# Fused two-layer conditional block on Trainium2: moving the raw score pairs from a batch's first half-steps to its later ones

## The chip, the cores and the metric

One Trainium2 chip, one of its cores. The metric is device time in microseconds (us) of one execution. TensorE is called PE, VectorE DVE, ScalarE ACT, GpSimd POOL, and SyncE (which issues most DMAs) SP.

## What is computed

The input is x (8 batches, 512 tokens, width 256) and a condition vector per batch. Two layers follow each other:

```
layer 0:  h = x * (scale(cond) * rsqrt(mean(x*x)+eps)); u = h @ up_w.T; val, gate = split(u)
          y = act_quant(val * gelu(gate)) @ weight_quant(down_w).T + x
layer 1:  x = y + a_alpha * attention(gamma * rmsnorm(y) + beta)          # 16 heads of 16
          out = x + f_alpha * (silu(n @ gate_w.T) * (n @ hidden_w.T) @ out_w.T + out_b),
                n = gamma' * rmsnorm(x) + beta'
```

Attention is softmax(q k^T / 4) v over all 512 keys.

## The kernel before

**Phase 1** is layer 0, tile by tile (32 tiles of 128 tokens). It ends near 262 us and the change does not touch it.

**Phase 2** is layer 1, one batch after the other. A batch is a table of 32 half-steps, h = 0 to 31 (HALVES). The heads are worked in four groups g of four heads; eight half-steps make a group, and two half-steps a tile of 128 keys. In every half-step PE does an *excursion* (excursion_pe, L1218): two score matmuls (score_pe, L923; keys by queries, 512 columns) for the softmax of the current batch, and the two halves of one *raw pair* (raw_pe, L882). A raw pair is the product of q and k for 128 queries of two heads without any shift, into the one two-bank PSUM tensor raw_pair. DVE reduces it to row maxima (maximum_dve, L890), and eight raw pairs (RAWS) complete a group: shift_dve (L896 to L902) turns the maxima into rows, and SP writes them with eight small DMAs into two rows of q_stack (shift_sp, L912), so that the score matmul subtracts the maximum itself. There is only one raw_pair tensor: raw_pe of pair n waits until DVE has read pair n-1 (raw_read). A score matmul uses 50 rows of the array in one half of it, and the raw half beside it 48 rows of the other half; the code alternates halves (1 - x).

Raw pairs run ahead of the scores: half-step h works on pair h + AHEAD, and AHEAD is 11; pair 32 is pair 0 of the next batch. Pair 16 is the first of the second pair of groups: it needs all twelve stacking DMAs of the batch (semaphore stacked[1]; eight issued by SP, four by ACT in h = 2 and 3, stack_act).

In the even half-steps PE also does values_pe (L942, probabilities times values of the previous key tile). Behind the excursion stands the half-step's entry in the table (plan, L1162): h 0 q and k projection of the second stack (qk_pe, L808); h 1 and h 4 the two halves of the value product (v_pe, L858, V_AT); h 2 and 3 the output projection of the batch before (wo_pe, L1003); h 7 the transposes of its normalised rows (xf_pe, L1059); h 8 and 9 q and k of the first stack of the next batch; h 10 to 25 alternately gate and hidden product of its feed-forward part (hidden_pe, L1091); h 26 to 31 its out product (out_pe, L1135, six entries of 12 or 24 matmuls). Every entry uses one of the two banks ab, whose release (pair_free) by DVE it waits for.

The other engines follow the same table one half-step later, each in its own fixed order. Around the change:

- DVE h 5: mean_dve (L1034), then the maximum, then normed_dve (L1044, four tensor_scalar of 128x256 that write the normalised rows for the transposes of h 7; semaphore xn3_done). v_dve (L865) copies a value half out of its bank first thing in the half-step after the product; xf_dve (L1068) follows the transposes in h 8 and waits for q_in_low, the split of the next batch's input, since both use x_in.
- ACT h 5: split_xa_act (L531) after the exps (exp_act, L931); POOL h 5: rstd_pool (L1038), split_xa_pool (L545). The place is SPLIT_XA_AT = V_AT[1] + 1. xf_act and xf_pool (L1081) and bias_pool (L1051) come at h 8.
- DVE h 8n: sums_dve (L955), h 8n+1: divide_dve (L961, L964); gate_dve (L1103) and product_dve (L1110) finish each gate and hidden product, and product_dve of a half-step stands before its maximum.

Batch 0 has no feed-forward part before it; its odd half-steps without an entry hold three filler matmuls (fill_pe, L1208). Batches 1 to 5 are a loop, 6 and 7 are written out; batch 7 has no following batch, so its raw pairs end with h 20. After it comes a tail for its own feed-forward part. Batches 1 to 6 are called the loop batches here.

Of the kernel before, what the change touches and what calls it, by code (L numbers as in the profile page):

```python
# [5 lines left out]
def cond_seq_kernel(nc, x_tok, xT, condT, vec_wT, up_wT, down_wT, wqT, wkT, wvT, woT, gate_wT, hidden_wT,  # L6
# [25 lines left out]
    G = 4  # L32
# [14 lines left out]
    with ctx:  # L47
# [161 lines left out]
        xn3_done = sem("xn3_done")  # L209
# [660 lines left out]
        def raw_at(b, n):  # L870

            return b + n // (RAWS * G), n % (RAWS * G) // RAWS, n % RAWS

        def raw_pe(pe, b, g, e, half):

            slot, qt = 2 * g + e // T, e % T
            if half == 1:
                if e == 0 and g % 2 == 0:
                    pe.wait_ge(stacked[g // 2], (b + 1) * STACK)
                pe.wait_ge(raw_read, credited(raw_read, b * (RAWS * G) + (RAWS * g + e)))  # L880
            rows = slice(64 * half, 64 * half + ROWS)
            mm = nc.tensor.matmul(raw_pair[:, half, :], q_stack[rows, slot, qt * P:(qt + 1) * P],  # L882
                                  k_stack[rows, slot, :], start=True, stop=True)
            if half == 0:
                mm.then_inc(raw_full, 1)
# [266 lines left out]

        V_AT, WO_AT, XF_AT, FFN_AT, OUT_AT = (1, 4), 2, 7, 10, 26
        Q_AT, K_AT, TO_STACK = 8, 9, 16
        SPLIT_XA_AT = V_AT[1] + 1
        OUT_PIECES = ([(0, 0)], [(2, 0)], [(0, 1)], [(1, 0), (1, 1)], [(2, 1)], [(3, 0), (3, 1)])
# [3 lines left out]
        def plan(ffn, following):  # L1162

            table = [[] for _ in range(HALVES)]
            table[0] = [("qk", 1, 0), ("qk", 1, 1)]
            for m in range(2):
                table[V_AT[m]] = [("v", m)]
            if following:
                table[Q_AT] = [("qk", 0, 0)]
                table[K_AT] = [("qk", 0, 1)]  # L1170
            if ffn:
                table[WO_AT] = [("wo", 0), ("wo", 1)]
                table[WO_AT + 1] = [("wo", 2), ("wo", 3)]
                table[XF_AT] = [("xf",)]
                for f in range(NH):
                    table[FFN_AT + 2 * f] = [("gate", f)]
                    table[FFN_AT + 2 * f + 1] = [("hidden", f)]
                for n, pieces in enumerate(OUT_PIECES):
                    table[OUT_AT + n] = [("out", t, half) for t, half in pieces]
            return table  # L1180
# [12 lines left out]
        def both(u, stage):  # L1193

            return tuple(u + n for n in stage)
# [15 lines left out]
        BEFORE = 1  # L1211
        USES_FIRST, USES_LOOP = uses(False, 2)[1], uses(True, 2)[1]

        def last_of(b, g):

            return (b, g - 1) if g > 0 else (b - 1, G - 1)

        def excursion_pe(pe, b, h, following):  # L1218

            g, kt = h // 2 // T, h // 2 % T  # L1220
            rb, rg, e = raw_at(b, h + AHEAD)
            raws = following or h + AHEAD < RAWS * G
            for x in range(2):
                score_pe(pe, b, g, kt, 2 * (h % 2) + x)
                if raws:
                    raw_pe(pe, rb, rg, e, 1 - x)

        def pe_batch(pe, b, u, ffn, following):
            table, at = plan(ffn, following), uses(ffn, following)[0]
            for h in range(HALVES):  # L1230
                excursion_pe(pe, b, h, following)
                n = h // 2
                if h % 2 == 0 and (n > 0 or ffn):
                    pb, pg = last_of(b, n // T) if n % T == 0 else (b, n // T)
                    values_pe(pe, pb, pg, (n - 1) % T, both(u, at["v"]) if n in (1, 1 + HALF) else None)
                if not ffn and not table[h] and h % 2 == 1:
                    fill_pe(pe, h, u, at)
                for p in table[h]:
                    if p[0] == "qk":
                        qk_pe(pe, b if p[1] == 1 else b + 1, p[1], p[2], u + at[f"qk{p[1]}"][p[2]])  # L1240
                    elif p[0] == "v":
                        v_pe(pe, b, p[1], u + at["v"][p[1]])
                    elif p[0] == "wo":
                        wo_pe(pe, b - 1, p[1], u + at["wo"][p[1] // HALF])
                    elif p[0] == "xf":
                        xf_pe(pe, b - 1, both(u, at["xf"]))
                    elif p[0] == "out":
                        out_pe(pe, b - 1, p[1], p[2], u + at["out"])
                    else:
                        hidden_pe(pe, b - 1, 0 if p[0] == "gate" else 1, p[1], u + at["hidden"])  # L1250
# [33 lines left out]

        def dve_batch(dve, b, u, ffn, following):
            table, at = plan(ffn, following), uses(ffn, following)[0]
            for h in range(HALVES + 1):
                g = h // 2 // T
                done = table[h - 1] if h > 0 else []
                for p in done:  # L1290
                    if p[0] == "v":
                        v_dve(dve, b, p[1], u + at["v"][p[1]])
                    elif p == ("qk", 1, 1):
                        qk_dve(dve, 1, 1, 4 * b + 2)
                    elif p[0] == "wo" and p[1] % HALF == HALF - 1:
                        wo_dve(dve, b - 1, p[1] // HALF, u + at["wo"][p[1] // HALF])
                        if p[1] == T - 1:
                            x2_dve(dve, b - 1, 1, u + at["wo"][1])
                    elif p[0] == "xf":
                        xf_dve(dve, b - 1, both(u, at["xf"]), b + 2 if following else b + 1)  # L1300
                    elif p[0] == "hidden":
                        product_dve(dve, b - 1, p[1], u + at["hidden"])
                    elif p[0] == "out" and p[1] % HALF == HALF - 1 and p[2] == 1:
                        out_dve(dve, b - 1, p[1] // HALF, u + at["out"])
                if ffn and h == WO_AT + 3:
                    mean_dve(dve, b - 1)
                if h < HALVES and (following or h + AHEAD < RAWS * G):
                    rb, rg, e = raw_at(b, h + AHEAD)
                    maximum_dve(dve, rb, rg, e)
                    if e == RAWS - 1:  # L1310
                        shift_dve(dve, rb, rg)
                if ffn and h == WO_AT + 1:
                    x2_dve(dve, b - 1, 0, u + at["wo"][0])
                if ffn and h == WO_AT + 3:
                    normed_dve(dve, b - 1)
                for p in done:
                    if p[0] == "gate":
                        gate_dve(dve, b - 1, p[1])
                    elif p[0] == "qk" and p[1] == 0:
                        qk_dve(dve, 0, p[2], 4 * b + 4)  # L1320
                if h < HALVES and h % 8 == 0 and (g > 0 or ffn):
                    sums_dve(dve, *last_of(b, g))
                if h == 0 and ffn:
                    divide_dve(dve, *last_of(b, g))
                if h == 0:
                    qk_dve(dve, 1, 0, 4 * b + 2)
                if h == 0 and ffn:
                    turn_dve(dve, b - 1, GP - 1)
                if h % 8 == 1 and g > 0:
                    divide_dve(dve, b, g - 1)  # L1330
                if h % 8 == 2 and g == 2:
                    turn_dve(dve, b, 0)

        def pool_batch(pool, b, u, ffn, following):
            table, at = plan(ffn, following), uses(ffn, following)[0]
            for h in range(HALVES + 1):
                g = h // 2 // T
                done = table[h - 1] if h > 0 else []
                if ffn and h == 1:
                    normalise_pool(pool, b - 1, GP - 1)  # L1340
                if g == 2 and h % 8 == 2:
                    normalise_pool(pool, b, 0)
                if ffn and h == WO_AT + 3:
                    rstd_pool(pool, b - 1)
                if following and h == SPLIT_XA_AT:
                    split_xa_pool(pool, b + 1)
                if ffn and h == XF_AT + 1:
                    xf_pool(pool, b - 1)
                    bias_pool(pool, b - 1)
                for p in done:  # L1350
                    if p[0] == "hidden":
                        product_pool(pool, b - 1, p[1])
                    elif p[0] == "out" and p[1] % HALF == HALF - 1 and p[2] == 1:
                        out_pool(pool, b - 1, p[1] // HALF, u + at["out"])
# [201 lines left out]
```

## Time and profile before

| | us |
|---|---|
| median of 3 runs | 1066.9 (1066.33 to 1073.98) |
| the profiled execution | 1072.98 |
| its span, first to last instruction | 1071.2 |
| mean granted clock of TensorE in it | 0.952 |
| PE busy / DVE busy / ACT busy / POOL busy | 1004.5 / 759.0 / 537.0 / 271.8 |

Busy shares are means over stages with different limits. The granted clock is a share of 2.4 GHz and has two levels here, 1.0 and 0.5. All start times below are us from the first instruction. Records of one engine overlap by about 0.1 us, so the step from one start to the next is the better price.

### The profile page before, as it was taken

What the parts mean: (1) busy time and instruction counts of PE and PEld (TensorE: products, weight loads), DVE (VectorE), ACT (ScalarE), POOL (GpSimd) and SP (SyncE); (2) the same over time, 40 slices, a digit from 0 to 9 for tenths busy, and PEclk for the clock granted to TensorE, in tenths of its full rate; (3) what the DMA queues carried; (4) which work ended last, traced back from release to release, by engine and by line L of the source; (5) the groups of instructions that cost most, each with busy time, mean ns of one, the idle gap of its engine ahead of it and who ended that gap; (6) DMA issues with size and microseconds to landing.
All of it is one profiled execution on the core that took longest, in us unless ns stands there. A gap on an engine that the chain in (4) does not pass through costs nothing.

```text
span 1071.2 us, 17062 instructions
## 1 busy us (share of the span) xinstructions
PE 1004.5 (94%) x5380; PEld 619.5 (58%) x5380; DVE 759.0 (71%) x1208; ACT 537.0 (50%) x1119; POOL 271.8 (25%) x260
## 2 busy tenths in 40 slices
PE   5999999996999899999989999998999899999868
PEld 4777777774434455545645564565556456645656
DVE  5888788995667786777577767867776776785232
ACT  4466455443555555446355535644564564456221
POOL 1265422220000321222122213212221321122133
PEclk9999999996999899979989998999999899999879
DMA  9545574442321220313024031302221230310000
GB/s 285 136 103 131 139 163 113 109 104 60 109 61 42 69 66 2 79 50 64 13 67 106 8 78 51 65 11 69 71 43 45 66 65 3 80 36 1 25 0 21
DMA packets 93685, 75.11 MB, mean 70 GB/s; under 512 B 44848, under 2 KB 79736, under 8 KB 93632
## 3 DMA queue, kind: packets, MB, share of 16 engines
q1 hardware_dynamic: 79040, 57.20, 20.4%
q10 hardware_dynamic: 14592, 17.25, 6.9%
q8 instruction: 27, 0.44, 0.2%
q14 instruction: 26, 0.21, 0.1%
HBM read 27.73 MB, written 12.61 MB: 38 GB/s over the span
## 4 chain that ended last, share of the span: by engine, by line
PE 81%; DVE 10%; issue 4%; DMA 2%; SPq 1%; ACT 1%; POOL 0%; DVEq 0%; POOLq 0%; ACTq 0%
PE bank L1091 19%; PE bank L358 13%; PE bank L923 11%; PE bank L942 10%; PE bank L1135 9%; PE raw_pair L882 5%; PE bank L808 5%; DVE rowmax L890 3%; PE bank L1003 3%; PE bank L381 2%; DVE amax L440 1%; PE bank L858 1%; PE bank L1059 1%; DVE x_in L1044 1%; SPq L912 1%
## 5 line engine op out<-in xcount | busy, mean ns | idle before, releaser
L890 DVE TENSOR_REDUCE rowmax<-raw_pair 128x2 f32<-128x1024 f32 x256 | 312.9, 1222 | 132.3 <-PE raw_pair L882 132.3
L931 ACT ACTIVATE probs<-bank 128x512 f32<-128x512 f32 x512 | 281.7, 596 | 231.3 <-PE bank L923 229.4
L923 PE MATMUL bank<-q_stack,k_stack 50*128 50x512 f32 x512 | 198.2, 458 | 2.4 <-DMA q_stack<-shift_rows 1.3
L358 PE MATMUL bank<-up_w,xs_part 128*128 128x512 f32 x768 | 193.8, 405 | 6.7 <-issue 5.3
L882 PE MATMUL raw_pair<-k_stack,q_stack 48*128 48x512 f32 x512 | 178.1, 472 | 21.9 <-DVE rowmax L890 21.3
L358 PEld LDWEIGHTS bank<-up_w,xs_part 128*128 128x128 f32 x768 | 143.7, 192 | 41.9 <-issue 8.5
L942 PE MATMUL bank<-probs,v_ext 128*17 128x512 f32 x1024 | 141.9, 627 | 0.3
L1121 POOL TENSOR_TENSOR hid<-scratch,hid 128x512 fp32r<-128x512 f32 x64 | 82.5, 1288 | 225.9 <-ACT hid L1117 225.9
L923 PEld LDWEIGHTS bank<-q_stack,k_stack 50*128 50x128 f32 x512 | 82.0, 191 | 88.1 <-issue 52.5
L1091 PE MATMUL bank<-xf_part,gate_w 128*128 128x512 f32 x384 | 108.0, 417 | 4.9 <-POOL xf_part L1081 4.2
L1091 PEld LDWEIGHTS bank<-xf_part,gate_w 128*128 128x128 f32 x384 | 68.8, 192 | 68.2 <-issue 51.5
L1135 PEld LDWEIGHTS bank<-out_w,hid 128*128 128x128 f32 x768 | 91.9, 188 | 25.6 <-issue 25.0
L1091 PE MATMUL bank<-xf_part,hidden_w 128*128 128x512 f32 x384 | 106.7, 413 | 0.0
L1135 PE MATMUL bank<-out_w,hid 128*128 128x256 f32 x768 | 100.6, 285 | 0.0
L882 PEld LDWEIGHTS raw_pair<-k_stack,q_stack 48*128 48x128 f32 x512 | 71.7, 191 | 41.1 <-DVE rowmax L890 36.3
L1091 PEld LDWEIGHTS bank<-xf_part,hidden_w 128*128 128x128 f32 x384 | 68.6, 190 | 33.0 <-issue 20.4
L288 ACT ACTIVATE gelu<-bank,rstd 128x512 f32<-128x512 f32 x64 | 44.0, 688 | 58.7 <-PE bank L358 58.7
L1099 ACT ACTIVATE scratch<-bank 128x512 f32<-128x512 f32 x64 | 38.2, 597 | 67.9 <-PE bank L1091 67.9
L410 DVE SCALAR_TENSOR_TENSOR h<-bank,rstd,gelu 128x512 f32<-128x512 f32 x64 | 47.7, 746 | 23.0 <-PE bank L358 23.0
L336 POOL TENSOR_TENSOR xs_part<-xs,xs_part 128x256 fp32r<-128x256 f32 x32 | 23.6, 739 | 147.1 <-DVE ms L403 126.7
L1103 DVE SCALAR_TENSOR_TENSOR scratch<-scratch,bank 128x512 f32<-128x512 f32 x64 | 43.4, 679 | 21.3 <-ACT scratch L1099 21.3
L982 POOL TENSOR_TENSOR split<-o_sb,split 128x512 fp32r<-128x512 f32 x16 | 20.5, 1282 | 130.5 <-ACT split L978 130.5
(121 smaller groups left out, 1108.6 us busy)
## 6 DMA issues: line engine op xcount, KB each, us to landing
q_stack<-split SPq DMA_DIRECT2D x48, 128.0 KB, 2.9
q_stack<-hid SPq DMA_DIRECT2D x48, 128.0 KB, 2.9
xk<-xT SPq DMA_DIRECT2D x32, 128.0 KB, 2.9
xt<-x_tok SPq DMA_DIRECT2D x32, 128.0 KB, 2.7
x_spill<-x1t ACTq DMA_DIRECT2D x32, 128.0 KB, 2.5
xa_spill<-xa ACTq DMA_DIRECT2D x32, 128.0 KB, 2.3
x_in<-xa_spill SPq DMA_DIRECT2D x8, 512.0 KB, 4.9
k_stack<-split ACTq DMA_DIRECT2D x32, 128.0 KB, 4.8
```

The source lines that it names most:

```text
L288: nc.scalar.activation(gelu[:, j, :], gate_bank[j][:], ACT.Gelu, scale=rstd[:, m % 2:m % 2 + 1]) \
L358: last = nc.tensor.matmul(bank[j][:], xs_part[a][:, m % 2, k, :], up_w[w][:, k, col + j * W:col + (j + 1) * W], start=(i == 0), stop=(i == ...
L410: nc.vector.scalar_tensor_tensor(h[:, j * W:(j + 1) * W], val_bank[j][:], rstd[:, m % 2:m % 2 + 1], gelu[:, j, :], ALU.mult, ALU.mult) \
L808: last = nc.tensor.matmul(bank[:], weight[wp][:, k, m * P:(m + 1) * P], xa_part[a][:, k, :], start=(i == 0), stop=(i == 5))
L882: mm = nc.tensor.matmul(raw_pair[:, half, :], q_stack[rows, slot, qt * P:(qt + 1) * P], k_stack[rows, slot, :], start=True, stop=True)
L890: nc.vector.reduce_max(rowmax[:, e:e + RAWS + 1:RAWS], raw_pair[:], AX.X).then_inc(raw_read, 1)
L923: nc.tensor.matmul(score_bank[c % 3][:], k_stack[rows, slot, kt * P:(kt + 1) * P], q_stack[rows, slot, :], start=True, stop=True).then_inc ...
L931: nc.scalar.activation(probs[:, (kt % 2) * J + j, :], score_bank[c % 3][:], ACT.Exp).then_inc(exp_done, 1)
L942: last = nc.tensor.matmul(o_bank[32 * j:32 * j + HD + 1, :], v_ext[:, kt, J * g + j, :], probs[:, (kt % 2) * J + j, :], start=(kt == 0), s ...
L1091: last = nc.tensor.matmul(ab[n][:], weight[wp][:, k, f * P:(f + 1) * P], xf_part[a][:, k, :], start=(i == 0), stop=(i == 5))
L1121: nc.gpsimd.tensor_tensor(hid[1][:, f, :], scratch[1][:], hid[0][:, f, :].bitcast(f32), ALU.subtract) \
L1135: last = nc.tensor.matmul(ab[m][:, (t % HALF) * D:(t % HALF + 1) * D], hid[a][:, f, t * P:(t + 1) * P], out_w[wp][:, f, :], start=(i == 0) ...
```

## The change

Three edits.

1. Raw pairs get a table of their own. None in h 0 to 4 and in h 6; two in h 12 and in h 22, 24, 26, 28 and 30; one in all others. Since each batch now starts with pair 16, a batch hands the next one 16 finished pairs rather than 11. In batch 0 the half-steps 0 to 4 keep theirs (the table starts at 11), so it does 37 raw pairs; batch 7 does 16. The first pair of a half-step stays inside the excursion; the second comes after values_pe, both halves one behind the other, ahead of the table's entry.
2. The second value product moves from h 4 to h 5, and with it v_dve to h 6 and the input split (ACT and POOL) from h 5 to h 6.
3. normed_dve moves from h 5 to h 6, and POOL's split waits for it.

```
-        V_AT, WO_AT, XF_AT, FFN_AT, OUT_AT = (1, 4), 2, 7, 10, 26
+        V_AT, WO_AT, XF_AT, FFN_AT, OUT_AT = (1, 5), 2, 7, 10, 26
+        RAW_PAIRS = [0] * 5 + [1, 0] + [1] * 5 + [2] + [1] * 8 + [1, 2] * 5 + [1]
+        def raw_table(first, following):
+            pairs = [1] * (2 * RAWS - AHEAD) + RAW_PAIRS[2 * RAWS - AHEAD:] if first else RAW_PAIRS
+            start = AHEAD if first else 2 * RAWS
+            table = [list(range(start + sum(pairs[:h]), start + sum(pairs[:h + 1]))) for h in range(HALVES)]
+            return [[n for n in numbers if following or n < RAWS * G] for numbers in table]
...
-        def excursion_pe(pe, b, h, following):
+        def excursion_pe(pe, b, h, raws):
             g, kt = h // 2 // T, h // 2 % T
-            rb, rg, e = raw_at(b, h + AHEAD)
-            raws = following or h + AHEAD < RAWS * G
             for x in range(2):
                 score_pe(pe, b, g, kt, 2 * (h % 2) + x)
-                if raws:
-                    raw_pe(pe, rb, rg, e, 1 - x)
+                for n in raws[:1]:
+                    raw_pe(pe, *raw_at(b, n), 1 - x)
...
                     values_pe(pe, pb, pg, (n - 1) % T, both(u, at["v"]) if n in (1, 1 + HALF) else None)
+                for n in raws[h][1:]:
+                    for half in (1, 0):
+                        raw_pe(pe, *raw_at(b, n), half)
...
-                if h < HALVES and (following or h + AHEAD < RAWS * G):
-                    rb, rg, e = raw_at(b, h + AHEAD)
+                for n in raws[h] if h < HALVES else []:
+                    rb, rg, e = raw_at(b, n)
                     maximum_dve(dve, rb, rg, e)
...
-                if ffn and h == WO_AT + 3:
+                if ffn and h == WO_AT + 4:
                     normed_dve(dve, b - 1)
...
                 if following and h == SPLIT_XA_AT:
+                    if ffn:
+                        pool.wait_ge(xn3_done, b)
                     split_xa_pool(pool, b + 1)
```

## Rows read from the trace of the kernel before

**Rows 1.** The page: busy time, and the group of the exps.

```profile
PE 1004.5 (94%) x5380; PEld 619.5 (58%) x5380; DVE 759.0 (71%) x1208; ACT 537.0 (50%) x1119; POOL 271.8 (25%) x260
...
L931 ACT ACTIVATE probs<-bank 128x512 f32<-128x512 f32 x512 | 281.7, 596 | 231.3 <-PE bank L923 229.4
```

**Rows 2.** Windows, first and last of six loop batches: length, busy per engine, granted clock, DMA share, GB/s.

```profile
338.79:435.80 97.01, 93.47 (x532) 53.59 (x528) 70.54 (x94) 50.01 (x97) 23.02 (x17) 0.95 0.21 52
...
822.68:918.28 95.60, 92.12 (x533) 52.79 (x529) 70.64 (x94) 49.74 (x98) 23.68 (x18) 0.96 0.20 50
```

**Rows 3.** Windows inside one loop batch (h 0 at 532.00, gate product at 567.00).

```profile
548.16:556.00 7.84, 4.55 (x21) 1.70 (x21) 6.48 (x10) 3.71 (x6) 3.46 (x2) 0.75 0.01 2
556.00:567.00 11.00, 11.00 (x50) 5.54 (x49) 7.64 (x10) 5.83 (x11) 4.88 (x3) 0.71 0.20 58
567.00:628.84 61.84, 61.84 (x362) 36.14 (x358) 43.16 (x56) 31.80 (x60) 12.83 (x10) 1.00 0.18 44
```

**Rows 4.** Timeline, same batch, h 4 to 8: start, length, instruction, idle before it.

```profile
546.54 1.69 PE L858 MATMUL bank<-wv,xa_part 128*128 128x256 f32 x12
...
548.16 0.73 PE L882 MATMUL raw_pair<-k_stack,q_stack 48*128 48x512 f32 x2
...
548.55 0.66 DVE L865 TENSOR_SCALAR v_ext<-bank 128x512 f32<-128x512 f32 x1
...
549.67 1.06 ACT L531 ACTIVATE xa_part<-x_in 128x1024 fp32r<-128x1024 f32 x1
550.42 3.24 DVE L1044 TENSOR_SCALAR x_in<-x,rstd 128x256 f32<-128x256 f32 x4
...
550.48 0.59 PE L882 MATMUL raw_pair<-k_stack,q_stack 48*128 48x512 f32 x2 [1.34 <-DVE rowmax L890]
...
550.81 2.44 POOL L545 TENSOR_TENSOR xa_part<-x_in,xa_part 128x1024 fp32r<-128x1024 f32 x1 [0.42 <-ACT xa_part L531]
...
554.85 0.88 PE L882 MATMUL raw_pair<-k_stack,q_stack 48*128 48x512 f32 x2 [1.95 <-DVE rowmax L890]
...
558.32 1.53 DVE L1068 TENSOR_SCALAR x_in<-bank,par 128x512 f32<-128x512 f32 x2 [0.95 <-PE bank L1059]
```

**Rows 5.** Timeline of batch 7: no input split; no raw pairs after h 20.

```profile
934.75 1.14 DVE L1044 TENSOR_SCALAR x_in<-x,rstd 128x256 f32<-128x256 f32 x4
...
943.96 2.28 DVE L964 TENSOR_TENSOR o_pair<-o_tok,inv_sum 128x256 f32<-128x256 f32 x1
...
976.17 0.49 PE L923 MATMUL bank<-q_stack,k_stack 50*128 50x512 f32 x2
976.59 1.67 PE L1091 MATMUL bank<-xf_part,hidden_w 128*128 128x512 f32 x6
```

**Rows 6.** Timeline of batch 0, three half-steps of its second half.

```profile
316.29 0.50 PE L882 MATMUL raw_pair<-k_stack,q_stack 48*128 48x512 f32 x2
...
318.37 0.51 PE L882 MATMUL raw_pair<-k_stack,q_stack 48*128 48x512 f32 x2
```

```profile
317.08 1.23 DVE L890 TENSOR_REDUCE rowmax<-raw_pair 128x2 f32<-128x1024 f32 x1 [0.85 <-PE raw_pair L882]
```

**Rows 7.** Timeline of the loop batch, h 24, in the feed-forward stretch.

```profile
604.08 0.49 PE L923 MATMUL bank<-q_stack,k_stack 50*128 50x512 f32 x1
...
604.75 1.05 PE L942 MATMUL bank<-probs,v_ext 128*17 128x512 f32 x8
605.73 1.66 PE L1091 MATMUL bank<-xf_part,gate_w 128*128 128x512 f32 x6
```

```profile
605.08 1.22 DVE L890 TENSOR_REDUCE rowmax<-raw_pair 128x2 f32<-128x1024 f32 x1
606.22 0.70 DVE L955 STREAM_TRANSPOSE o_tok<-bank 128x512 f32<-128x512 f32 x1
```

**Rows 8.** ACT's last stacking DMA, and issue to landing in us.

```profile
544.01 0.61 ACTq L829 DMA_DIRECT2D k_stack<-hid  x1
```

```profile
k_stack<-hid ACTq DMA_DIRECT2D x2, 128.0 KB, 3.7
```

More of the change, by code:

```diff
@@ L1212, in cond_seq_kernel @@
         USES_FIRST, USES_LOOP = uses(False, 2)[1], uses(True, 2)[1]
+        RAW_PAIRS = [0] * 5 + [1, 0] + [1] * 5 + [2] + [1] * 8 + [1, 2] * 5 + [1]
[4 more added lines that the diff above has]
+            return [[n for n in numbers if following or n < RAWS * G] for numbers in table]
         def last_of(b, g):
             return (b, g - 1) if g > 0 else (b - 1, G - 1)
-        def excursion_pe(pe, b, h, following):
+        def excursion_pe(pe, b, h, raws):
             g, kt = h // 2 // T, h // 2 % T
-            rb, rg, e = raw_at(b, h + AHEAD)
-            raws = following or h + AHEAD < RAWS * G
             for x in range(2):
                 score_pe(pe, b, g, kt, 2 * (h % 2) + x)
-                if raws:
-                    raw_pe(pe, rb, rg, e, 1 - x)
+                for n in raws[:1]:
+                    raw_pe(pe, *raw_at(b, n), 1 - x)
         def pe_batch(pe, b, u, ffn, following):
             table, at = plan(ffn, following), uses(ffn, following)[0]
+            raws = raw_table(not ffn, following)
             for h in range(HALVES):
-                excursion_pe(pe, b, h, following)
+                excursion_pe(pe, b, h, raws[h])
                 n = h // 2
@@ L1286, in dve_batch @@
             table, at = plan(ffn, following), uses(ffn, following)[0]
+            raws = raw_table(not ffn, following)
             for h in range(HALVES + 1):
```

## The prediction, made before the changed kernel was run

> **What bounds the kernel now.** I read the page first: PE is busy 94% of the span [rows 1], so what counts is where PE waits and at which clock it runs. Windows cut at each batch's first projection give the periods: the six loop batches lie between 338.79 and 918.28, so 96.6 us each on average, the first 97.01 and the last 95.60 [rows 2]. Windows inside one loop batch then show two stretches. From the gate product (h 10) to the next batch PE is busy all 61.84 us at clock 1.00: nothing waits there, and whatever is added to PE's order is paid in full. From h 5 to the transposes of h 7 PE is busy only 4.55 of 7.84 us, and the granted clock is 0.75 there and 0.71 in the 11.00 us after: part of both ran at 1.2 GHz [rows 3]. So all there is to gain lies between h 0 and h 10. That stretch takes 567.00 - 532.00 = 35.0 us in this batch, and on average 96.6 - 61.8 = 34.8.
>
> The timeline names the causes [rows 4]. PE's raw matmuls wait 1.34 us in h 6 and 1.95 in h 7 for DVE to have read the raw pair before. DVE is late because four maxima, the residual work and the normalisation (L1044) stand in one queue. That normalisation takes 3.24 us beside POOL's split (L545, 2.44 us); in batch 7, which has no split, the same four instructions take 1.14 [rows 5]. After these waits the clock is at 1.2 GHz.
>
> **The change part by part, in a loop batch.** PE prices come from steps between starts. An excursion with a raw pair takes 604.75 - 604.08 = 0.67 us and values_pe 0.98 [rows 7]; two scores without a raw pair take 976.59 - 976.17 = 0.42 [rows 5], since they then run side by side. So leaving a raw pair out gives PE only 0.25 us: the pair was nearly hidden behind the scores. A projection or gate product is 1.6 [rows 7], the second value product 548.16 - 546.54 = 1.62 [rows 4].
>
> *Early half-steps.* In h 0 to 4 five pairs go: 5 x 0.25 = 1.25 us. In the new order h 5 starts where the old h 4 began its value product, at 546.54 - 1.25 = 545.3 on the old batch's scale. There stands pair 16, which needs the last stacking DMA. ACT issued it at 544.01, 3.7 us before landing [rows 8]; its half-step now comes some 0.8 us sooner, so it lands near 543.2 + 3.7 = 546.9. The old order arrived at 548.16 and did not wait [rows 4]; the new one waits about 1.3 us after its first score, and the value product stands behind it. This is the wait that the change adds. PE: rest of the excursion and value product, 546.9 + 0.7 + 1.6 = 549.2. The rest is a chain of one engine after the other: v_dve 0.66 [rows 4] with its release, to 550.0; meanwhile ACT does h 6's two exps (2 x 0.6 [rows 1]), to 550.9; ACT's split 1.06 to 552.0; POOL's split 2.44 to 554.4; xf_dve 1.53 to 555.9 [rows 4]. The normalisation now takes 1.14 and is done near 551.2, ahead of POOL's start, so the new POOL wait costs nothing and is what keeps the two apart. The transposes of h 7 are no longer late. Late next is the q projection of h 8, whose bank xf_dve must free: PE gets there near 554.7 and waits 1.2 us. From 555.9 to the gate product stand two projections, two excursions and one values_pe: 3.2 + 1.34 + 0.98 = 5.5, so 561.4 against 567.00: 5.6 us gained in this batch, 34.8 - 29.4 = 5.4 on average, at full clock. Bounds: had PE no wait at all, the same rows add up to some 25.3 us of work, a gain of 9.5; with the clock down after the 1.3 us wait, a gain of 3.
>
> SP's queue is passed without cost: shift rows of group 1 are now ready at the end of the batch before and stand behind the eight stacking DMAs, but are used only in h 8; group 0's are ready two half-steps sooner. The v_dve of h 2 may hold values_pe for 0.4 us, in place of the wait for DVE that stood there.
>
> *Doubles.* A second pair has no score beside it (0.42 us by the two scores alone) and must wait until DVE has read the first. Batch 0 shows that cycle free of other work: raw start to raw start 318.37 - 316.29 = 2.08 us, with DVE starting 0.79 after the raw and taking 1.23 [rows 6]. In a double half-step PE reaches the second pair after 0.67 + 0.98 = 1.65, so it stands 0.45, and the double costs 0.45 + 0.42 = 0.87. Where product_dve comes first it is more: in h 24 DVE began the maximum 1.00 after PE's start and was free at 606.22, 2.14 after it [rows 7], so 0.6 + 0.42 = 1.0 in h 12, 22 and 24. Behind h 24's second maximum DVE has the sums (0.70 [rows 7]), h 25's maximum, which ends some 6.35 us behind h 24's start, then gate, reciprocal with division, and product of h 26, at about 0.65 each: 8.3. h 26 itself begins at 0.67 + 0.98 + 0.6 + 0.42 + 1.6 + 0.67 + 1.6 = 6.5; its first maximum ends at 9.4, PE reaches the second pair at 8.2 and stands 1.2: 1.6 in all. Together: 3 x 1.0 + 1.6 + 2 x 0.87 = 6.4 us, all in the stretch where PE never waits. Bounds: 6 x 0.42 = 2.5, if DVE were always in time, and 6 x 1.6 = 9.6.
>
> A loop batch so loses 6.4 - 5.4 = 1.0 us; six of them: **+6**.
>
> **Batch 0** keeps its early pairs and does 37 instead of 32. Its second half runs at one raw cycle, 2.08 us, per half-step [rows 6]: PE has less work than that, so each further pair costs a whole cycle. Five pairs: +10.4; back to back halves can shorten a cycle to perhaps 1.85, +9.3. The double of h 12 costs 2.0 more, and h 6 without a pair and the moved value product give back 1.3. **+11**. Two half-steps then hold about 4.3 us of PE work (two excursions, values_pe, a bare pair, and some 0.9 for the filler, half a projection's matmuls) in three cycles, 6.1, with waits of 0.45 and 1.2 us close together, in the range of the waits after which the clock fell in rows 4. I add **+2.5** for one or two falls.
>
> **Batch 7** gains what the loop batches do early, without the split in the way, but it lost less before: its normalisation already took 1.14 [rows 5]. The same chain without split and q projection gives about -2.8 (an estimate), h 12's double +1.0: **-2**.
>
> The tail is the same. Sum: 6 + 11 + 2.5 - 2 = +17.5 us on the execution's 1073.0, so 1090.5. That execution stood 6.1 above the median of the runs; on the median, 1066.9 + 17.5 = 1084.4, I say **1085**.
>
> **A rule of the notes against one term.** In batch 7 the division L964, over 256 elements a partition, took 2.28 us while POOL added the bias [rows 5], longer than a maximum over 1024 [rows 6]. The Trainium skill, SBUF — State Buffer, section Who interferes with whom, says that a VectorE instruction with two SBUF inputs contends with a GpSimd one that reads SBUF, and that the one that issues first holds the shared ports for its whole length. By that rule, the trace agrees. The new order moves xf_dve, and so the bias addition behind it, towards the division of h 9, which it can then block: rival C.
>
> **Rivals.**
> *A, not slower.* The doubles always meet a free DVE (0.87 each, 5.2 per batch), the stacking lands 1.4 us sooner than I think because its issues moved up, and the wait in h 8 shrinks by 0.7: -5.4 - 1.4 - 0.7 + 5.2 = -2.3 per loop batch, -14; batch 0 +10.5 with no clock loss, batch 7 -3.5: -7, so 1060. It decides where pair 16 is found landed within 0.4 us. For it: the clock loss is real and stays away for certain only if both early waits do. Against: the landing time in rows 8 and the full PE in rows 3. Chance 0.2.
> *B, the clock falls again,* in h 5 or behind h 24 to 26, where PE stands 1.2 to 1.3 us. Some 6.8 us at 1.2 GHz (rows 3: 0.71 over 11 us is 6.4 us at half) in a stretch full of PE work costs 3.4 us a batch, +20: 1105. For it: waits of 1.34 and 1.95 brought it before. Against: these are single and shorter. Chance 0.25.
> *C, the port.* The division of h 9 takes up to the 2.28 us of rows 5 in each loop batch; PE has one gate product to spare (1.6), so the maximum that it needs in h 11 is up to 1 us late: +6, 1091. For it: rows 5. Against: the division lay just clear of the bias in the loop batches before, and most of the delay is covered. Chance 0.1.
> The forecast keeps 0.45. That the change does not do what it says, with the early waits left as they are, can be excluded only by the counts: the pairs leave h 0 to 4 by the table, so I give it nothing.
>
> **How the numbers follow.** A measurement of this kernel tells about 1% from no change (10.7 us): the bounds are 1056.2 and 1077.6. Slower: B and C, 0.35, and 0.33 of the forecast's 0.45: 0.68. Same: the rest of it, 0.12, and 0.14 of A: 0.26. Faster: 0.06, of A, if early waits and doubles both come out at their low bounds. The range reaches from A to B: 1061 to 1104.
>
> **What would show it.** In the profile after: batch 0 longer by 11 to 14 us, with maxima back to back every 2 us through h 22 to 31; loop batches of 96 to 99; L1044 at 1.2 us; a wait at pair 16 for a DMA (k_stack), a wait at the q projection for xf_dve (x_in L1068); raw matmuls that wait 0.4 to 0.6 and 1.2 us in the doubles; clock 1.00 from h 5 to h 10. Wrong if the loop batches are under 94 us, or if batch 0 grows by less than 8.

## The result, and the profile after

The changed kernel takes 1117.4 us, median of 4 runs (1112.3 to 1122.3), against 1066.6 for the kernel before: a ratio of 1.046, 95% interval 1.039 to 1.053. Slower was the likelier side of the forecast, but 1085 was far too little, and 1117 lies outside the range of 1061 to 1104.

The profiled execution took 1119.03 us, its span 1117.2 at a mean granted clock of 0.956. The page first, engines and the group of the raw matmuls (idle before them at the end of each line, by releaser):

```profile
PE 1015.1 (91%) x5377; PEld 622.0 (56%) x5377; DVE 751.0 (67%) x1208; ACT 537.7 (48%) x1119; POOL 271.0 (24%) x260
...
L882 PE MATMUL raw_pair<-k_stack,q_stack 48*128 48x512 f32 x512 | 169.4, 479 | 47.1 <-DVE rowmax L890 31.5
```

PE is busy about as long as before (1015 against 1004 [rows 1]) in a span 46 us longer, so 35 of the 46 went into idle time of PE. The list of waits names most of it (us in all, times, longest); of the kernel before first, of the changed one second:

```profile
PE raw_pair L882 <- DVE rowmax L890: 21.3, 15, 2.3
```

```profile
PE raw_pair L882 <- DVE rowmax L890: 31.5, 47, 1.3
PE raw_pair L882 <- DMA k_stack<-hid: 14.9, 8, 2.6
...
PE bank L808 <- DVE x_in L1068: 5.7, 6, 1.4
```

The waits for DVE are three times as many and shorter, and there is a new one, once in each of the eight batches, for the stacking DMAs.

To place the 46 us I cut both executions at each batch's first q projection (1.6 us behind the h 0 of the forecast's stretches) and at each first gate product (h 10); "early" lies between the two, "late" after the gate product:

| us | before | after | difference | forecast |
|---|---|---|---|---|
| start of batch 0 | 263.62 | 264.73 | +1.1 | 0 |
| batch 0 | 75.17 | 94.43 | +19.3 | +13.5 |
| six loop batches, early part | 33.13 each | 30.37 each | -16.5 | -32.4 |
| six loop batches, late part | 63.45 each | 70.43 each | +41.9 | +38.4 |
| batch 7 and tail | 152.9 | 153.2 | +0.3 | -2 |
| span | 1071.2 | 1117.2 | +46.0 | +17.5 |

The windows of after behind this table: batch 0 whole and in two parts, then a loop batch early and late, and its early part from pair 16 on (length, busy time of PE, PEld, DVE, ACT, POOL, granted clock, DMA share, GB/s):

```profile
264.73:359.16 94.43, 84.47 (x354) 35.20 (x352) 56.09 (x68) 42.22 (x73) 3.65 (x2) 0.81 0.20 49
289.60:321.94 32.34, 30.64 (x137) 12.38 (x133) 22.32 (x30) 16.41 (x29) 1.27 (x1) 0.89 0.31 70
321.94:359.16 37.22, 31.74 (x117) 10.82 (x116) 21.20 (x25) 12.81 (x22) 0.00 (x0) 0.69 0.01 2
561.98:591.28 29.30, 26.42 (x154) 14.77 (x150) 17.55 (x28) 17.49 (x37) 10.44 (x7) 0.94 0.32 76
591.28:661.73 70.45, 66.64 (x382) 37.61 (x378) 51.69 (x66) 32.76 (x62) 13.13 (x11) 1.00 0.17 42
...
576.16:591.28 15.12, 14.38 (x77) 6.94 (x77) 10.52 (x16) 9.28 (x16) 7.67 (x5) 0.89 0.07 25
```

Two things stand out. The late part runs at clock 1.00 throughout: its 7 us are the doubles alone. Batch 0 runs at 0.81 as a whole and at 0.69 from h 22 on. Now the timeline of a loop batch, h 5 to 8, against [rows 4]:

```profile
571.84 0.66 ACTq L829 DMA_DIRECT2D k_stack<-hid  x1
...
574.06 0.49 PE L923 MATMUL bank<-q_stack,k_stack 50*128 50x512 f32 x1
576.16 0.61 PE L882 MATMUL raw_pair<-k_stack,q_stack 48*128 48x512 f32 x2 [1.61 <-DMA k_stack<-hid]
...
576.82 1.90 PE L858 MATMUL bank<-wv,xa_part 128*128 128x256 f32 x12
...
579.44 1.13 DVE L1044 TENSOR_SCALAR x_in<-x,rstd 128x256 f32<-128x256 f32 x4
...
580.45 1.06 ACT L531 ACTIVATE xa_part<-x_in 128x1024 fp32r<-128x1024 f32 x1
...
581.59 2.36 POOL L545 TENSOR_TENSOR xa_part<-x_in,xa_part 128x1024 fp32r<-128x1024 f32 x1 [5.00 <-ACT xa_part L531]
...
584.24 1.53 DVE L1068 TENSOR_SCALAR x_in<-bank,par 128x512 f32<-128x512 f32 x2 [0.70 <-POOL xa_part L545]
...
585.82 1.65 PE L808 MATMUL bank<-xa_part,wq 128*128 128x512 f32 x6 [0.53 <-DVE x_in L1068]
```

The predicted chain is there, link by link: pair 16 waits for a DMA, the value product behind it, then v_dve, the two splits, x_in and the q projection. The normalisation takes 1.13 us instead of 3.24, and the q projection waits 0.53 us. But pair 16 starts 4.3 us after the last stacking DMA's issue (571.84 to 576.16), for a landing after 3.7 in the forecast [rows 8], and the clock of the 15.12 us behind it is 0.89.

### The profile page after: what moved, and what is told of

Its sections match the earlier page's. It is cut to its first block, busy times and chain, and to the rows that moved or that the text cites. A ratio compares the mean times of both kernels' runs of the same rounds, so it can differ in the third digit from the quotient of the medians.

```text
span 1117.2 us, 17067 instructions
## 1 busy us (share of the span) xinstructions
PE 1015.1 (91%) x5377; PEld 622.0 (56%) x5377; DVE 751.0 (67%) x1208; ACT 537.7 (48%) x1119; POOL 271.0 (24%) x260
## 4 chain that ended last, share of the span: by engine, by line
PE 52%; DVE 18%; issue 17%; POOL 6%; DMA 4%; ACT 1%; ACTq 0%; SPq 0%; DVEq 0%; POOLq 0%
PE bank L358 11%; PE bank L1135 8%; PE bank L1091 7%; DVE rowmax L890 7%; PE bank L923 5%; PE raw_pair L882 5%; PE bank L942 4%; DMA k_stack<-hid 3%; PE bank L858 3%; PE bank L808 3%; POOL hid L1121 2%; DVE amax L440 2%; PE bank L1003 2%; POOL xa_part L545 1%; DVE h L410 1%
## 5 line engine op out<-in xcount | busy, mean ns | idle before, releaser
L882 PE MATMUL raw_pair<-k_stack,q_stack 48*128 48x512 f32 x512 | 169.4, 479 | 47.1 <-DVE rowmax L890 31.5
L923 PE MATMUL bank<-q_stack,k_stack 50*128 50x512 f32 x512 | 189.0, 472 | 1.1 <-issue 1.1
L882 PEld LDWEIGHTS raw_pair<-k_stack,q_stack 48*128 48x128 f32 x512 | 67.6, 190 | 107.3 <-DVE rowmax L890 85.2
L923 PEld LDWEIGHTS bank<-q_stack,k_stack 50*128 50x128 f32 x512 | 76.8, 192 | 89.4 <-issue 53.5
```

What stands on the lines that cost most here:

```text
L923: nc.tensor.matmul(score_bank[c % 3][:], k_stack[rows, slot, kt * P:(kt + 1) * P], q_stack[rows, slot, :], start=True, stop=True).then_inc ...
```

## The experiments

Each kernel ran on one chip beside the kernel before, whose median was 1065.1 us beside e1 to e4, 1066.5 beside e5 to e8 and 1066.1 beside e9 to e11. A ratio is to it, with its 95% interval. b0, early and late are the cuts of the table above, in the one execution profiled of each kernel. The first theory was that the new waits, at pair 16 and in batch 0, with the clock behind them, are what the forecast lacks.

| run | what it has | us | ratio | b0 | early | late |
|---|---|---|---|---|---|---|
| before | | 1066.6 | | 75.2 | 33.1 | 63.45 |
| after | all three edits | 1117.4 | 1.046 | 94.4 | 30.4 | 70.4 |
| e1_pairs_alone | edit 1 | 1110.8 | 1.041 [1.038, 1.044] | 94.2 | 29.9 | 70.5 |
| e2_order_alone | edits 2 and 3 | 1049.7 | 0.985 [0.982, 0.987] | 75.2 | 29.7 | 63.5 |
| e3_pool_wait_alone | before, POOL's wait | 1049.4 | 0.984 [0.981, 0.987] | 75.4 | 29.6 | 63.4 |
| e4_pair16_in_h6 | after, pair 16 in h 6 | 1095.6 | 1.029 [1.026, 1.033] | 91.5 | 27.2 | 70.5 |
| e5_fill_batch0 | after, fillers in batch 0 | 1106.2 | 1.037 [1.035, 1.038] | 87.3 | 31.7 | 70.5 |
| e6_sp_after_stack | after, SP's order | 1120.2 | 1.049 [1.045, 1.052] | 93.3 | 30.8 | 70.5 |
| e7_pair_inside_entry | e4, second pair later | 1092.8 | 1.025 [1.023, 1.026] | 94.2 | 27.5 | 70.1 |
| e8_one_pair_moved | edits 2, 3, one pair moved | 1055.6 | 0.990 [0.988, 0.991] | 79.0 | 28.8 | 64.6 |
| e9_pairs_and_pool_wait | edit 1, POOL's wait | 1096.9 | 1.030 [1.028, 1.031] | 94.2 | 27.1 | 70.5 |
| e10_split_later_alone | before, split in h 6 | 1050.6 | 0.987 [0.985, 0.989] | 75.2 | 29.1 | 63.4 |
| e11_pair16_h6_filled | e4 and e5 together | 1086.5 | 1.020 [1.018, 1.021] | 84.0 | 27.2 | 70.5 |

### The parts of the change by themselves

e1 is the changed kernel with edits 2 and 3 undone:

```
-        V_AT, WO_AT, XF_AT, FFN_AT, OUT_AT = (1, 5), 2, 7, 10, 26
+        V_AT, WO_AT, XF_AT, FFN_AT, OUT_AT = (1, 4), 2, 7, 10, 26
...
-                if ffn and h == WO_AT + 4:
+                if ffn and h == WO_AT + 3:
                     normed_dve(dve, b - 1)
...
-                    if ffn:
-                        pool.wait_ge(xn3_done, b)
```

> The table of raw pairs alone; the value product, the normalisation and the split stand where they were before, and POOL does not wait. If the loss comes from the doubles, batch 0's longer raw cycle and the clock (theory 1), most of it stays: some +17 us in batch 0 and +7 late in each loop batch, less 3 to 5 early, 1090 to 1105 us in all; pair 16 no longer waits for the stacking DMAs, since the value product stands ahead of it, and the normalisation takes 3.2 us again. If the later chain of value product, split and xf_dve eats the early gain (theory 2), this kernel keeps that gain, 7 us a batch, and comes to 1085 us or less.

e2 is the changed kernel with the table of raw pairs undone (excursion_pe and dve_batch as before), e3 the kernel before with nothing but

```
                 if following and h == SPLIT_XA_AT:
+                    if ffn:
+                        pool.wait_ge(xn3_done, b)
                     split_xa_pool(pool, b + 1)
```

> One raw pair in every half-step as before; only the value product in h 5, the normalisation and the split in h 6, and POOL's wait. Theory 1: the normalisation takes 1.14 us and DVE is less late, pair 16 waits about 1 us for the stacking DMAs; loop batches 1 to 2 us shorter than before, 1055 to 1062 us. Theory 2 (this later chain costs the early gain): loop batches 1 us or more longer, 1073 us or more.

> The kernel before with nothing but POOL's wait for the normalisation ahead of its split. If the 3.2 us of the normalisation were the sharing with the split, it takes 1.14 us now and the raw wait of h 7 (1.95 us) goes; the split ends about 0.8 us later, and xf_dve with it: 1 to 2 us less per loop batch, 1054 to 1062 us. Rival: the later split holds xf_dve and the projection behind it by as much as DVE gains: 1066 us, no change.

Measured: 1110.8, 1049.7 and 1049.4. All three fell outside what was expected of them, e1 slower, the others faster. The pair table alone costs 46 us; edits 2 and 3 without it gain 15 to 17, and POOL's wait alone gains all of it. The timeline of e3, h 6 and 7, shows how:

```profile
540.89 1.14 DVE L1044 TENSOR_SCALAR x_in<-x,rstd 128x256 f32<-128x256 f32 x4
540.95 0.58 PE L882 MATMUL raw_pair<-k_stack,q_stack 48*128 48x512 f32 x2 [1.31 <-DVE rowmax L890]
...
542.19 2.36 POOL L545 TENSOR_TENSOR xa_part<-x_in,xa_part 128x1024 fp32r<-128x1024 f32 x1 [1.33 <-DVE x_in L1044]
543.23 0.59 PE L882 MATMUL raw_pair<-k_stack,q_stack 48*128 48x512 f32 x2
```

The first wait, 1.31 us in h 6, is still there [rows 4: 1.34]. The second, 1.95 in h 7, is gone. In this batch the clock does not fall either. In two of e3's six loop batches it stays at 1.00 (early parts of 28.3); in the other four the same first wait is there and the early part runs at 0.89 to 0.94 and takes 29.2 to 31.0. The window of this batch's early part:

```profile
524.17:552.43 28.26, 26.76 (x164) 15.43 (x161) 23.76 (x37) 17.27 (x36) 10.21 (x7) 1.00 0.31 73
```

If the parts added up, after would stand at +46 - 15 = +30. It stands at +51 by the medians: 20 us come from the table and edits 2 and 3 meeting each other.

### What meets: pair 16 and the value product

```
-        RAW_PAIRS = [0] * 5 + [1, 0] + ...
+        RAW_PAIRS = [0] * 5 + [0, 1] + ...
```

> The changed kernel with pair 16 moved from h 5 to h 6, so that the second value product stands ahead of it. Theory 1 (the wait for the stacking DMAs, 1.6 to 2.6 us, and the clock after it cost the early gain): the wait at pair 16 is gone, loop batches 2 to 3 us shorter than in the changed kernel, batch 0 too, 1097 to 1105 us. Rival: its maximum now stands ahead of the normalisation and delays it and the transposes by 1.2 us, so PE waits there instead: 1112 us or more.

Measured: 1095.6, a little under what was expected, and 21.8 less than after. With pair 16 a half-step later, behind the value product, no wait for the DMA is left, the clock stays at 1.00 and the early part falls from 30.4 to 27.2. But that moves a raw pair too. e9 takes the other side of the meeting away: the table and POOL's wait, with the value product left in h 4 and the normalisation in h 5.

> The pair table alone (value product in h 4, normalisation in h 5, as in the kernel before) with one thing more: POOL's split waits for the normalisation. In the run of the table alone the early part of a loop batch took 29.9 us, with a normalisation of 3.23 us beside POOL's split, transposes that stood 1.89 us for it, and 1.2 GHz after that. Theory: the table and the shared time of DVE and POOL are separate things, so the wait is worth here too what it is worth in the kernel before, 3.5 us at most, 1.2 us for the step of the transposes alone: early parts of 27.0 to 28.5, time 1094 to 1103 against 1110.8. Rival: with the pairs gone from h 0 to 4 the early part is a chain value product, split, split, x_in, and a split that starts later only moves its end: early parts stay at 29.5 to 30.5, time 1109 to 1114.

Measured: 1096.9, early 27.1, as the theory said. Its timeline, h 4 and 5:

```profile
560.93 0.71 ACTq L829 DMA_DIRECT2D k_stack<-hid  x1
...
563.14 1.70 PE L858 MATMUL bank<-wv,xa_part 128*128 128x256 f32 x12
564.76 0.50 PE L923 MATMUL bank<-q_stack,k_stack 50*128 50x512 f32 x1
...
565.26 0.61 PE L882 MATMUL raw_pair<-k_stack,q_stack 48*128 48x512 f32 x2
```

Pair 16 again starts 4.3 us after the last stacking DMA's issue, but the product stood in front of it and filled that time, and no wait is left to be listed in this batch. The early part of this batch runs at clock 1.00:

```profile
551.09:578.24 27.15, 25.32 (x155) 14.70 (x151) 17.48 (x28) 17.42 (x37) 10.48 (x7) 1.00 0.36 82
```

The sums and means of the windows of all six early parts, of after and of e9, show what the 3.3 us a batch (30.37 - 27.11) consist of:

```profile
sum 182.24, PE 161.61 PEld 93.75 DVE 105.37 ACT 104.59 POOL 61.84; mean PE 26.94 PEld 15.63 DVE 17.56 ACT 17.43 POOL 10.31
```

```profile
sum 162.63, PE 151.56 PEld 88.10 DVE 104.79 ACT 104.35 POOL 61.87; mean PE 25.26 PEld 14.68 DVE 17.47 ACT 17.39 POOL 10.31
```

PE is busy 26.94 us a batch for 25.26, the same work at a lower clock: the granted clock is 0.88 to 0.94 in each of after's six early parts and 1.00 in each of e9's. It is idle 3.4 us for 1.8. So 1.7 us are the clock and 1.6 the wait, and six times 3.3 is the 20. The value product behind pair 16 (edit 2), which gains nothing without the table (e2 beside e3), costs 20 us with it; e4, which keeps edits 2 and 3 and moves only the pair, gets the same 20 back.

Is it SP's queue that makes the landing 4.2 and not 3.7? e6 lets SP issue the shift rows only when the stacking has landed:

```
+            sp.wait_ge(stacked[1], (b + 1) * STACK)
             shift_sp(sp, b, 1)
```

> The changed kernel where SP issues the shift rows of group 1 only when all twelve stacking DMAs have landed. If these eight small DMAs, which now fall among the stacking ones, lengthened ACT's last landing from 3.7 to 4.2 us, it is 3.7 again, pair 16 waits 0.5 us less and a loop batch is 0.5 to 1 us shorter: 1110 to 1114 us. Rival: the landing is longer because the stacking DMAs themselves come closer together: still 4.2 us and no change, 1117.

Measured: 1120.2, no gain, and pair 16 still starts 4.4 us after the issue, in e6's timeline:

```profile
667.76 0.62 ACTq L829 DMA_DIRECT2D k_stack<-hid  x1
672.16 0.65 PE L882 MATMUL raw_pair<-k_stack,q_stack 48*128 48x512 f32 x2 [1.70 <-DMA k_stack<-hid]
```

The shift rows are not it. Counted from the batch's first q projection, ACT issues its last stacking DMA 9.9 us in, 0.5 sooner than before (10.4), but it lands 14.1 us in, as before (14.0): the landing did not follow the issue. That the stacking DMAs, now closer together, delay one another is left as the likely cause; it was not tried by itself.

### Batch 0

```
                     for half in (1, 0):
                         raw_pe(pe, *raw_at(b, n), half)
+                    if not ffn:
+                        for i in range(FILL):
+                            nc.tensor.matmul(ab[0][:], wo[0][:, i % GP, 0:P], ...)
```

The fillers write a bank that nobody reads at that time, as the kernel's own do. The execution profiled of e5 stood 10.4 us above its median, so only its batch 0 is read, and not its early parts of 31.7.

> The changed kernel with three more filler matmuls behind each second pair of batch 0, where PE stands about 1.1 us; nothing else differs. If batch 0 grew by more than its raw cycles because the clock fell there (1.2 GHz in much of h 22 to 31), the fillers keep it up and each pair of half-steps falls from 6 to 8 us towards 6.0: batch 0 shrinks from 94.4 to 87 to 90 us and the whole to 1110 to 1113. Rival: the clock has no part, fillers only add work: batch 0 94 us or more, the whole 1117 or more.

Measured: 1106.2, 4 us less than expected, batch 0 at 87.3, as expected. Of the 11 us less than after, 7.2 are batch 0; the others are not placed. The timeline of after: the first and the second pair of h 22, the pair of h 23, both of h 24 and that of h 25:

```profile
322.48 0.50 PE L882 MATMUL raw_pair<-k_stack,q_stack 48*128 48x512 f32 x2
...
324.56 0.50 PE L882 MATMUL raw_pair<-k_stack,q_stack 48*128 48x512 f32 x2 [0.37 <-DVE rowmax L890]
...
326.38 0.51 PE L882 MATMUL raw_pair<-k_stack,q_stack 48*128 48x512 f32 x2 [1.08 <-DVE rowmax L890]
...
328.47 0.51 PE L882 MATMUL raw_pair<-k_stack,q_stack 48*128 48x512 f32 x2
...
331.08 0.79 PE L882 MATMUL raw_pair<-k_stack,q_stack 48*128 48x512 f32 x2
...
333.20 0.80 PE L882 MATMUL raw_pair<-k_stack,q_stack 48*128 48x512 f32 x2 [0.90 <-DVE rowmax L890]
```

At 2.4 GHz three cycles take 5.99 us (322.48 to 328.47), the 6.1 of the forecast. At 1.2 GHz (the same matmuls take 0.80 and not 0.50) they took 7.83 (333.20 to 341.03), in steps of 2.73, 2.98 and 2.12, of which only the last has a wait (0.90): in the other two PE's own work, at half the clock, is longer than the cycle. In e5 the clock stays up, with PE busier:

```profile
320.00:360.00 40.00, 37.56 (x182) 18.43 (x182) 25.29 (x34) 16.98 (x30) 1.27 (x1) 1.00 0.15 34
```

So the clock costs batch 0 at least 7.2 us: that much came back although the fillers are work of their own. The unfilled batch 0 varies with it: e4, e7 and e9 differ from after there only in h 4 to 6, e4 and e7 not at all from each other, and they take 91.5, 94.2 and 94.2. The last window of e9's batch 0:

```profile
320.00:355.55 35.55, 30.66 (x101) 10.66 (x101) 19.29 (x23) 11.62 (x20) 0.00 (x0) 0.62 0.01 1
```

e9 saves after's wait of 2.55 us in h 5 of batch 0 and loses it again to a lower clock later. e11 takes both causes away in one kernel:

> The changed kernel with the two causes taken away together that were taken away one at a time: pair 16 in h 6, and three filler matmuls behind each second pair of batch 0. If they are separate terms, batch 0 takes 91.5 - 7.2 = 84.3 us, the early parts stay at 27.2, the late ones at 70.5, and the time is 1095.6 - 7.2 = 1088.4 (1085 to 1090). If they share a cause (the clock), less of it: batch 0 above 88, time 1092 to 1096.

Measured: 1086.5, batch 0 at 84.0, early 27.2, late 70.5: the two are separate terms. Batch 0 is 3.2 us under e5's, which has the fillers and still the wait (2.89 us there). What is left, 84.0 - 75.2 = 8.8 us at the same mean clock as before (0.97), is the added pairs. The time is close to the 1085 forecast, but in part by chance. Between the executions profiled it is +13.5 for +17.5: early parts 0.5 us a batch better (a gain of 5.9 for 5.4), late ones 0.6 worse, batch 0 4.7 better; and the execution of before stood 6.1 above its median.

### The doubles

e7 is e4 with the second pair of a loop batch's double inside the entry's product (`inside` issues both its halves) and not ahead of it, where PE still has work; e8 moves a single pair, from h 6 to h 12, on top of edits 2 and 3, 11 pairs ahead as before:

```
             for i, (a, wp, k) in enumerate(PROJECTION):
+                if inside is not None and i == 2:
+                    inside()
...
             for i in range(half * n, half * n + n):
                 a, wp, f = steps[i]
+                if inside is not None and i == half * n + 4:
+                    inside()
```

```
+        RAW_PAIRS = [1] * 6 + [0] + [1] * 5 + [2] + [1] * 19
```

> As e4 (pair 16 in h 6), and in batches 1 to 6 the second pair of h 12 and h 22 to 30 stands a third into the gate or out product instead of ahead of it, by when DVE has read the first. If a double costs PE 0.42 us of work and the rest is the wait (0.37 to 1.05 us), the late part of a loop batch falls from 70.6 to 67 to 68 us and the whole from 1095.6 to 1075 to 1083. Rival: the wait only moves behind, to the first pair of the next half-step: late part 70 us or more, 1092 or more.

> Order as in e2, and of the pairs only one moves: none in h 6, two in h 12, 11 ahead as before. By the price of a double in h 12, about 1.1 us in each of seven batches and 2 in batch 0, less 0.25 us and perhaps 0.5 of waits early, it is 2 to 7 us slower than e2 (1049.7): 1052 to 1057. Rival: the early part is so tight on DVE that the missing pair of h 6 gives back more than the double costs: 1047 or less.

e7 measured 1092.8, only 2.8 under e4, with 70.1 for 70.5 in the late part: the rival was right. Its timeline after a moved second pair:

```profile
616.78 0.50 PE L882 MATMUL raw_pair<-k_stack,q_stack 48*128 48x512 f32 x2
618.34 0.49 PE L923 MATMUL bank<-q_stack,k_stack 50*128 50x512 f32 x1
618.60 0.59 PE L882 MATMUL raw_pair<-k_stack,q_stack 48*128 48x512 f32 x2
```

The wait doesn't vanish. Part of it stays: the second pair starts at 616.78, when DVE has just read the first (until 616.72). The rest moves to the next half-step's pair, which starts 0.26 us behind its score and not beside it: a raw pair needs 1.8 us from the last (1.82 here), wherever it stands. e8 measured 1055.6, 5.9 above e2, as expected: late +1.1 per batch, batch 0 +3.8, early -0.85. One moved pair is a loss by itself.

### Is it the wait, or the separation, that pays in e3?

```
-        SPLIT_XA_AT = V_AT[1] + 1
+        SPLIT_XA_AT = V_AT[1] + 2
```

> The kernel before with the input split (ACT and POOL) in h 6 in place of h 5 and nothing else; no added wait. DVE's normalisation stays in h 5. Theory (what pays is that the two aren't at work at the same time, whoever is first): the normalisation falls from 3.24 to 1.14 us, the wait of 1.95 us in h 7 goes, and the time is 1048 to 1056, that of the run with POOL's wait alone (1049.4) or a little more, since POOL's split starts later. Rival (it is the order of DVE first, POOL directly behind, that pays; a later split makes x_in late by what it saves): 1060 to 1068.

Measured: 1050.6, with no wait added. The timeline of e10:

```profile
539.97 1.14 DVE L1044 TENSOR_SCALAR x_in<-x,rstd 128x256 f32<-128x256 f32 x4
...
542.42 2.37 POOL L545 TENSOR_TENSOR xa_part<-x_in,xa_part 128x1024 fp32r<-128x1024 f32 x1 [2.48 <-ACT xa_part L531]
```

Whatever keeps POOL's split off DVE's normalisation gives the 16 us. In the kernel before, where, in the batch shown, the split started at 550.81, 0.39 us behind the normalisation's first instruction [rows 4], three of the four instructions took 0.34 to 0.35 us each and one 2.45, as long as POOL's split (2.44), which itself lost nothing against the 2.36 of e3. In the view of that line's instructions of before, window 549 to 555 (min/median/max in ns):

```profile
L1044 DVE TENSOR_SCALAR x_in<-x,rstd x4: 341/348/2446, 550.4 to 553.3; 128x256 f32<-128x256 f32 x4
```

DVE's instruction was not slowed in proportion, it stood until POOL's ended (553.40 and 553.25). The Trainium skill, SBUF — State Buffer, section Who interferes with whom, says that an instruction of the tensor_scalar kind can hold the SBUF port pair that VectorE shares with GpSimd, and that the one issued first keeps it for its whole length. By that rule, the trace agrees.

## Why the prediction was wrong, step by step

The forecast missed by 28.5 us on the profiled executions (+46.0 for +17.5). Two steps carry most of it, the early gain of the loop batches and the clock in batch 0. The rest of the distance from 1085 to 1117 is that the execution profiled before stood 6.1 us above its median and the one after only 1.7.

- **The early half-steps, 15.9 of the 28.5.** "5.4 on average, at full clock" was the step that failed; 2.75 came. The links of the chain were all there, but the wait at its head was mis-sized: 1.61 us here and 1.7 on average ((14.9 - 2.55 - 2.11) / 6, without batches 0 and 7) for "about 1.3". The forecast let the landing come sooner with its issue, 3.7 us behind it; it took 4.2 and came no sooner than before. And the forecast ran the chain "at full clock", with the clock's fall only as the lower bound (a gain of 3) and as rival B. e4 and e9 show that the wait and the fall after it are worth 3.2 us a batch. Without them the gain is 6.0. The work behind the wait was a little over-priced: from pair 16 to the gate product the forecast has 561.4 - 546.9 = 14.5 us, and 15.12 were measured with PE at 0.89, where full speed would give back up to 1.7; the q projection waits 0.53 in the batch shown for "1.2".
- **The doubles, 3.5.** "6.4 us" a batch was measured as 7.0. By the waits of one batch, with 0.42 for each bare pair: h 12 1.07, h 22 1.16, h 24 0.97 (forecast 1.0 each), h 26 1.47 (1.6), h 28 and 30 0.79 each (0.87), 6.25 together. The steps hold. What they left out is the half-step behind a double: after h 26 the raw pair of h 27 starts 0.57 us behind its score, not beside it, since DVE is still reading the second pair. The timeline of after with the doubles of h 12, 22, 24, 26 and 28, and h 27's first score and raw pair (h 30 is as h 28):

```profile
597.50 0.50 PE L882 MATMUL raw_pair<-k_stack,q_stack 48*128 48x512 f32 x2 [0.65 <-DVE rowmax L890]
...
626.46 0.49 PE L882 MATMUL raw_pair<-k_stack,q_stack 48*128 48x512 f32 x2 [0.74 <-DVE rowmax L890]
...
633.02 0.50 PE L882 MATMUL raw_pair<-k_stack,q_stack 48*128 48x512 f32 x2 [0.55 <-DVE rowmax L890]
...
640.08 0.50 PE L882 MATMUL raw_pair<-k_stack,q_stack 48*128 48x512 f32 x2 [1.05 <-DVE rowmax L890]
...
642.08 0.50 PE L923 MATMUL bank<-q_stack,k_stack 50*128 50x512 f32 x1
...
642.65 0.58 PE L882 MATMUL raw_pair<-k_stack,q_stack 48*128 48x512 f32 x2
...
646.98 0.50 PE L882 MATMUL raw_pair<-k_stack,q_stack 48*128 48x512 f32 x2 [0.37 <-DVE rowmax L890]
```

- **Batch 0, 5.8.** "+11" at full clock was somewhat too much: e11, with fillers and no wait at pair 16, has +8.8. "I add +2.5 for one or two falls" failed: the clock costs at least 7.2 (e5), since h 22 to 31 run at a mean of 0.69, which is some 23 of their 37 us at 1.2 GHz. And pair 16's wait is in batch 0 too, 2.55 us, which I priced in the loop batches alone.
- **Batch 7, 2.3.** "-2" became +0.3. The early gain, -2.8 forecast, is -0.8: pair 16 waits there too, 2.11 us, in a batch without the split to gain from. The double is +1.1 for "+1.0".
- **Batch 0's start, 1.1.** Layer 0 is untouched in every run here, and batch 0 starts between 260.9 and 264.7 us in them: this is scatter.

**The rivals.** A (not slower) named its own point of decision, whether pair 16 is found landed, and it was not. B named the right mechanism, a fall of the clock, and one of its two places, h 5. Behind h 24 to 26 it never came: 1.00 over the whole 70.45 us. Its 1105 was too low, as it left batch 0 at +2.5 and the early wait at 1.3. C (the port) stayed small: the division of h 9 took 0.73 us in the loop batch shown, for 0.42 before, and in batch 7 2.25 for 2.28. SP's queue is passed without cost held (e6).

**What was right for a reason not named.** I read the early gain as the work of the whole change. e3 shows that 3.5 of the 6.0 us come from one wait on POOL, and would have come without moving a pair; emptying h 0 to 4 of five raw pairs and h 6 of a sixth brings only 2.5 more (e9 beside e3; where e3's clock stays at 1.00 too, 28.3 against 27.15, only 1.1), for the 7.0 that the doubles cost. In the forecast's own prices that could be read: a pair hidden beside a score costs PE 0.25 us, a bare one 0.42 and a wait. Six pairs moved from the one place to the other cannot pay unless a large wait goes with them, and the large wait that went was due to POOL.

## What to carry to other kernels

Work that runs beside other work on an engine is nearly free where it is; before moving it to relieve an early stretch, price it where it lands, bare and with the release that it must await, and the half-step behind it. Where two edits meet (here a product put behind an operation that awaits a DMA, in a table whose first pair is that operation), the sum of their separate prices is not the price: look for what used to stand in front of the waiting instruction and covered it. And when a vector instruction is three times as long in one stage as in another, separate it from GpSimd first: here that one wait was worth 1.6%, and nothing else that was tried gained more.

## What the runs showed of the hardware that I had not expected

- The clock fell behind short waits amid dense work. The loop batch shown of after stands 1.61 us at pair 16 and shows 0.89 over the next 15.12 us; its batch 0 stands 0.4 to 1.1 us six times in the last ten half-steps and shows 0.69 over 37.22 us. With three more matmuls behind each second pair the same stretch shows 1.00. The length of one wait does not decide it: e3 waits 1.2 to 1.3 us at the same place in each of its six loop batches, and four of them show a fall (0.89 to 0.94) and two none; e4 waits 1.5 us at the q projection of five loop batches and 1.25 at the sixth, and its clock stays at 1.00. The waits of up to 1.05 us in after's late parts were followed by none.
- Six more groups of fillers in batch 0, useless work, make that batch 7.2 us shorter (e5).
- One 128x256 tensor_scalar of four took 2.45 us in place of 0.35 beside a GpSimd tensor_tensor over 128x1024 that had started 0.14 us before it, and 0.35 in e3 and e10, where the two are apart.
- The same stacking DMAs take longer from issue to landing after the change, though neither their size nor their queues changed. The trace's lists of DMA issues, one loop batch each (KB each, median us from issue to landing), before and after:

```profile
k_stack<-hid ACTq DMA_DIRECT2D x4, 128.0 KB, 3.7
...
k_stack<-hid SPq DMA_DIRECT2D x2, 128.0 KB, 4.6
```

```profile
k_stack<-hid ACTq DMA_DIRECT2D x4, 128.0 KB, 4.2
...
k_stack<-hid SPq DMA_DIRECT2D x2, 128.0 KB, 4.9
```

The kernel to keep is neither of the two, but the kernel before with POOL's split kept off the normalisation: 1049.4 us by the wait (e3), 1050.6 by the later place (e10).
